# Graph layer kernel on one core: attention's q and k loads regrouped from half blocks to head parities

## The chip, the cores and the metric

The kernel runs on one core of a Trainium2 chip. The metric is the device time of one execution in microseconds (us), lower is better. The kernel before takes 2124.48 us (median of 3 runs, 2124.31 to 2126.77).

## The reference, cut to what matters

There are 6250 nodes with 512 features, 106250 edges sorted by their target, and 64 features per edge. In order:

```python
xn = layernorm(x)
agg = segment_sum(edge_attr, dst) / count            # edges into nodes
gnn = xn + relu(concat(xn, agg) @ W1 + b1) @ W2 + b2
q, k, v = split(xn @ W_qkv.T + b_qkv)                # 8 heads of 64
q, k = sigmoid(q), sigmoid(k)
# i, o, i_hat, o_hat: sums over all nodes of q and k, in two rounds
vw = v * softmax(o_hat, over nodes)
kv = einsum('bshd,bshe->bsde', k, vw)                # per node: heads x heads
r  = einsum('bshd,bsde->bshe', q / i, kv) * sigmoid(i_hat)
x1 = x + gnn + r.reshape(...) @ W_out.T + b_out
out = x1 + gate * expert(layernorm(x1))              # one expert of 16
```

Attention is local to a node: its 8 heads of q meet its own 8 heads of k, an 8x8 matrix per node that is scaled by `mix` (what the softmax, `i` and `i_hat` amount to) and applied to its own v.

## The kernel before, in words

The work goes through six stages one after the other: project (norm, q, k, v and W1's part that needs no edges), norms and scale (the sums over all nodes), attend, gnn, expert. Nodes are handled in 12 full blocks of 512 and a last one of 106 (`TAIL`). Beside the first four stages runs the edge work: SP (SyncE) loads batches of 1024 edges (`Edges.load`, L196, L198, L201: indices, the indices of the whole batch on every partition, attributes), DVE (VectorE) writes selection matrices (L237), PE (TensorE) sums (L249), ACT (ScalarE) copies (L262), and POOL (GpSimd) adds rows into tables in HBM with indirect DMAs of 128 rows (L297), 831 in all. There are 9 buffers (`KEPT`) between ACT and POOL.

Project writes q and k to the HBM tensor `qk_halves`, of shape side (q, k) x 25 half blocks x 128 x 4 chunks x 256 nodes. A feature's chunk is `o`, and the 128 partitions of a chunk are 2 parities `x` of heads times 64 features `d`; one `[o, t]` row of a feature and half block is 4096 contiguous bytes. Norms and scale read it by `load_halves` (L909), one transfer of 1024 KB for each side of a block, with the 128 features outermost on both sides: `rearrange("w p o t -> p w (o t)")`.

Attend (`attend_stage`, L1292) wants another layout. Its tiles `q` and `kk` are `[128, 8, 256]`: partitions 0 to 63 hold feature d of the block's first 256 nodes, partitions 64 to 127 those of the second 256, and the free dimension holds 8 heads (parity x, then chunk o) by 256 nodes. `load_qk` (L1385) fills them with four transfers a block, of 512 KB each: half 0 of q, half 0 of k, half 1 of q, half 1 of k. Each writes 64 partitions, 8192 bytes in each (two rows of 4096, one of either parity). All four count on `qk_in[b % 2]`, and ACT's `by_token` (L1559), which turns k into `kt` with the 8 heads of a node side by side (L1566), waits for the four at once. PE's `scores` (L1485) then multiplies 16 nodes by 16 nodes (128x128) of which DVE's `neighbours` (L1625) keeps the 8x8 blocks on the diagonal, times `mix`; `mixing` (L1509) applies v, and `output` (through `products`, L365) multiplies with W_out in three passes of fp32r. The last block takes TAIL nodes of one half with its own four transfers (L1395), on 64 partitions.

The order of SP's queue in attend is written out by hand (L1445 to L1469). For block b it is: one batch of edges; wait until block b-1 is scored; `load_qk(b + 1)`; wait until block b-1 is mixed; `load_v(b + 1)` (L1401); 16 small transfers for `mix` of block b+1 (L1373), each to 8 partitions, 8 KB in pieces of 32 bytes; the store of block b-1 (L1440); edges; `load_x(b + 1)` (L1411); edges. All of them go through SP's one DMA queue (q1), in order; POOL's indirect DMAs go through q0. Before the loop SP issues `load_qk(0)`, W_out, v of block 0, two biases (L1420, L1421), the stores of `mix` (L1425, L1428) and its first loads, then `load_qk(1)`. The q, k, v, x and mix tiles each have two buffers.

Transfers of the tail block with 106 nodes on the outermost side are L1414 (x), L1443 (store of attend) and L2283 (the last store of the kernel, L2280 for a full block).

Of the kernel before, what the change touches and what calls it, by code (L numbers as in the profile page):

```python
# [17 lines left out]
HDIM = DIM // HEADS  # L18
# [4 lines left out]
CH = DIM // P  # L23
QK = 2 * CH
JH = HID // P
BT = 512
HALF = BT // 2
FULL = TOKENS // BT
TAIL = TOKENS - FULL * BT
# [20 lines left out]
def subtiles(n):  # L50

    return [min(P, n - s) for s in range(0, n, P)]
# [824 lines left out]
def block_at(b):  # L877

    return slice(b * BT, min(TOKENS, (b + 1) * BT))
# [412 lines left out]
def attend_stage(nc, c, edges, before):  # L1292
# [5 lines left out]
    with ExitStack() as ctx:  # L1298
        def sb(what, shape, dt=F32):
            return ctx.enter_context(nc.sbuf_tensor(f"at_{what}", shape, dt))  # L1300
# [4 lines left out]
        def sem(what):  # L1305
            return c.whole.enter_context(nc.semaphore(f"at_{what}"))
# [6 lines left out]
        q, kk, v, x = [[sb(f"{what}0", shape)] for what, shape in  # L1313
                       (("q", [P, HEADS, BT // 2]), ("k", [P, HEADS, BT // 2]), ("v", [P, GROUPS, HDIM]),
                        ("x", [P, CH, DIM]))]
# [23 lines left out]
        mix_in, qk_in, v_in, x_in = [[sem(f"{what}_in{k}") for k in range(2)] for what in ("mix", "qk", "v", "x")]  # L1339
# [27 lines left out]
    def load_mix(b, eng, first, step=2):  # L1367
        part = [i for i, (g0, g1) in enumerate(MIX_PARTS) if g0 <= b * CH < g1][0]
        eng.wait_ge(mix_stored[part], 16)
        rows = c.mix[b * BT:b * BT + sizes[b], :]  # L1370
        for t, g in mix_loads(sizes[b])[first::step]:
            src = rows[t:t + (g - 1) * GT + 1:GT, :].rearrange("g (a h) -> a g h", a=HEADS)
            eng.dma_start(mix[b % 2][t * HEADS:(t + 1) * HEADS, 0:g, t * HEADS:(t + 1) * HEADS], src  # L1373
                          ).then_inc(mix_in[b % 2], 16)
# [8 lines left out]

    def sp_program(sp):
        def load_qk(b):  # L1385
            for half, r in enumerate([BT // 2, BT // 2] if b < FULL else [TAIL]):
                for side, dst in enumerate((q[b % 2], kk[b % 2])):
                    rows = slice(half * HDIM, (half + 1) * HDIM)
                    if r == HALF:
                        sp.dma_start(dst[rows, :, :].rearrange("d (x o) t -> d x (o t)", x=2),  # L1390
                                     c.qk[side, 2 * b + half, :, :, :].rearrange("(x d) o t -> d x (o t)", x=2)
                                     ).then_inc(qk_in[b % 2], 16)
                    else:
                        for x in range(2):
                            sp.dma_start(dst[rows, x * CH:(x + 1) * CH, 0:r],  # L1395
                                         c.qk[side, 2 * b, x * HDIM:(x + 1) * HDIM, :, 0:r]).then_inc(qk_in[b % 2], 16)

        def load_v(b):
            rows = c.v.rearrange("t (h e) -> (t h) e", h=HEADS)
            full = sizes[b] // GT  # L1400
            sp.dma_start(v[b % 2][:, 0:full, :], rows[b * BT * HEADS:b * BT * HEADS + full * P, :]  # L1401
                         .rearrange("(g p) e -> p g e", p=P)).then_inc(v_in[b % 2], 16)
            left = sizes[b] % GT * HEADS
            if left:
                at = b * BT * HEADS + full * P
                sp.dma_start(v[b % 2][0:left, full, :], rows[at:at + left, :]).then_inc(v_in[b % 2], 16)

        def load_x(b):
            n = sizes[b]
            if n == BT:  # L1410
                sp.dma_start(x[b % 2][:, :, :], c.x[block_at(b), :].rearrange("(s p) d -> p s d", p=P)  # L1411
                             ).then_inc(x_in[b % 2], 16)
            else:
                sp.dma_start(x[b % 2][0:n, 0, :], c.x[block_at(b), :]).then_inc(x_in[b % 2], 16)  # L1414

        sp.wait_ge(before.io_mm, EARLY_FREE)
        load_qk(0)
        weights.load(sp)
        load_v(0)
        sp.dma_start(bias[:, :], c.b2.partition_broadcast(P)).then_inc(bias_in, 16)  # L1420
        sp.dma_start(bias_out[:, :], c.b_out.partition_broadcast(P)).then_inc(bias_in, 16)  # L1421
        for i, (g0, g1) in enumerate(MIX_PARTS):
            sp.wait_ge(c.mix_ready, i + 1)
            if (g1 - 1) * P < TOKENS - P:
                sp.dma_start(c.mix[g0 * P:g1 * P, :].rearrange("(s p) f -> p s f", p=P), c.mix_sb[:, g0:g1, :]  # L1425
                             ).then_inc(mix_stored[i], 16)
            else:
                sp.dma_start(c.mix[g0 * P:TOKENS, :], c.mix_sb[0:TOKENS - g0 * P, g0, :]).then_inc(mix_stored[i], 16)  # L1428
            if i == 0:
                load_mix(0, sp, 0)  # L1430
        before.over(sp)
        load_qk(1)
        load_x(0)
        weights.wait(sp)

        def store(b):
            n = sizes[b]
            sp.wait_ge(acc_free, b * CH + len(subtiles(n)))
            if n == BT:
                sp.dma_start(c.base[block_at(b), :].rearrange("(s p) d -> p s d", p=P), done[b % 2][:, :, :]  # L1440
                             ).then_inc(stored[b % 2], 16)
            else:
                sp.dma_start(c.base[block_at(b), :], done[b % 2][0:n, 0, :]).then_inc(stored[b % 2], 16)  # L1443

        for b in range(NB):  # L1445
            batches = share.batches(b)
            for batch in batches[:1]:
                edges.load_ahead(sp, *batch)
            if b + 1 < NB:
                if b:  # L1450
                    sp.wait_ge(scored, b * STEPS)
                    load_qk(b + 1)
                    sp.wait_ge(mixed, b * STEPS)
                else:
                    sp.wait_ge(prepared, 1)
                load_v(b + 1)
                load_mix(b + 1, sp, 0, 1)
            if b:
                store(b - 1)
            for batch in batches[1:2]:  # L1460
                edges.load_ahead(sp, *batch)
            if b + 1 < NB:
                if b:
                    sp.wait_ge(rest_ready, b * CH)
                load_x(b + 1)
            for batch in batches[2:]:
                edges.load_ahead(sp, *batch)
        me.preload(sp)
        store(NB - 1)  # L1469
# [1079 lines left out]
```

## Time and profile before

| | |
|---|---|
| Median of 3 runs | 2124.48 us |
| Profiled execution, its own time | 2126.26 us |
| Its span, first to last instruction | 2124.5 us |
| PE, PEld (weight loads), DVE, POOL, ACT busy | 88%, 71%, 58%, 62%, 26% |
| Mean granted TensorE clock | 0.922 of full speed |
| SP's DMA queue q1, POOL's q0 | 369.74 MB and 28.99 MB |
| q and k loads of attend | 48 transfers of 512 KB |

The profile's page gives busy shares of a whole span; attend is the stretch from about 1094 to 1592 us. "SPq" is time in which SP's queue issues a DMA or is held up in issuing it; a DMA's packets are counted apart, as a share of the time of the core's 16 DMA engines, which can go over 1 where packets of two queues overlap on an engine.

### The profile page before, as it was taken

What the parts mean: (1) busy time and instruction counts of PE and PEld (TensorE: products, weight loads), DVE (VectorE), ACT (ScalarE), POOL (GpSimd) and SP (SyncE); (2) the same over time, 40 slices, a digit from 0 to 9 for tenths busy, and PEclk for the clock granted to TensorE, in tenths of its full rate; (3) what the DMA queues carried; (4) which work ended last, traced back from release to release, by engine and by line L of the source; (5) the groups of instructions that cost most, each with busy time, mean ns of one, the idle gap of its engine ahead of it and who ended that gap; (6) DMA issues with size and microseconds to landing.
All of it is one profiled execution on the core that took longest, in us unless ns stands there. A gap on an engine that the chain in (4) does not pass through costs nothing.

```text
span 2124.5 us, 31099 instructions
## 1 busy us (share of the span) xinstructions
PE 1875.1 (88%) x10776; PEld 1512.1 (71%) x10776; DVE 1222.8 (58%) x3872; ACT 560.4 (26%) x1314; POOL 1325.7 (62%) x850
## 2 busy tenths in 40 slices
PE   2799999999999999788776978888767999998798
PEld 1688888888888888544435767777655888887686
DVE  3643454443443432377855656465648888885575
ACT  1422333223332223111131121212123333333210
POOL 4888888888888888688888787777885000000100
PEclk9999999999999999866586998889887999999899
DMA  9977887777787777799799999999969666653884
GB/s 291 226 158 149 145 157 148 159 148 146 151 158 152 137 133 137 202 233 207 143 307 188 209 195 207 183 210 185 204 133 249 216 212 209 215 180 117 305 292 151
DMA packets 502384, 400.77 MB, mean 189 GB/s; under 512 B 356932, under 2 KB 369476, under 8 KB 502228
## 3 DMA queue, kind: packets, MB, share of 16 engines
q1 hardware_dynamic: 380164, 369.74, 60.5%
q0 software_dynamic: 119952, 28.99, 22.0%
q8 instruction: 86, 1.41, 0.3%
q14 instruction: 70, 0.57, 0.1%
q10 hardware_dynamic: 2112, 0.07, 0.1%
HBM read 244.05 MB, written 154.62 MB: 188 GB/s over the span
## 4 chain that ended last, share of the span: by engine, by line
PE 67%; SPq 17%; DMA 6%; DVE 6%; issue 2%; ACT 1%; POOL 0%; DVEq 0%; POOLq 0%; ACTq 0%
PE pr_out_bank L365 26%; PE gn_acc L365 12%; SPq L1373 9%; PE pr_v_bank L365 7%; PE edge_sum L249 6%; PE ex_y_bank L365 6%; SPq L1390 2%; PE at_acc L365 2%; PE nm_io_bank L872 2%; DMA done<-qk_halves 2%; SPq L196 1%; DVE nm_wide L1093 1%; DMA at_k<-qk_halves 1%; DVE edge_sel L237 1%; PE gn_h L1951 1%
## 5 line engine op out<-in xcount | busy, mean ns | idle before, releaser
L297 POOL DMA_INDIRECT table<-edge_ring,edge_row x831 | 1314.7, 1582 | 309.9 <-issue 226.3
L237 DVE SCALAR_TENSOR_TENSOR edge_sel<-edge_dst_all,edge_dst_f,upper 128x128 f32<-128x128 int16 x831 | 317.3, 438 | 92.3 <-PE edge_sum L249 61.2
L365 PE MATMUL pr_out_bank<-pr_norm_xT_hi,pr_w_hi 128*128 128x512 f32 (+1 forms) x832 | 327.8, 394 | 0.0
L365 PE MATMUL pr_out_bank<-pr_norm_xT_lo,pr_w_hi 128*128 128x512 f32 (+1 forms) x832 | 319.5, 384 | 0.0
L365 PE MATMUL pr_out_bank<-pr_norm_xT_hi,pr_w_lo 128*128 128x512 f32 (+1 forms) x832 | 318.7, 383 | 0.0
L249 PEld LDWEIGHTS edge_sum<-edge_attr,edge_sel 128*128 128x128 f32 x1662 | 236.9, 213 | 110.7 <-DVE edge_sel L237 80.3
L249 PE MATMUL edge_sum<-edge_attr,edge_sel 128*128 128x65 f32 x1662 | 244.3, 297 | 73.4 <-DVE edge_sel L237 71.7
L2292 POOL DMA_INDIRECT ex_w_raw<-in_w_exp,ex_row x4 | 5.2, 1295 | 337.0 <-issue 337.0
L262 ACT ACTIVATE edge_ring<-edge_sum 128x260 f32<-128x260 f32 (+1 forms) x209 | 80.3, 385 | 399.0 <-PE edge_sum L249 311.3
L365 PEld LDWEIGHTS pr_out_bank<-pr_norm_xT_lo,pr_w_hi 128*128 128x128 f32 x832 | 156.7, 188 | 32.1
L365 PEld LDWEIGHTS pr_out_bank<-pr_norm_xT_hi,pr_w_lo 128*128 128x128 f32 x832 | 157.1, 189 | 28.3
L365 PEld LDWEIGHTS pr_out_bank<-pr_norm_xT_hi,pr_w_hi 128*128 128x128 f32 x832 | 157.0, 189 | 27.8
L365 PE MATMUL gn_acc<-gn_w_hi,gn_h_hi 128*128 128x512 f32 (+1 forms) x392 | 155.7, 397 | 0.3 <-DVE gn_h_lo L2096 0.3
L365 PE MATMUL gn_acc<-gn_w_lo,gn_h_hi 128*128 128x512 f32 (+1 forms) x392 | 153.6, 392 | 0.0
L365 PE MATMUL gn_acc<-gn_w_hi,gn_h_lo 128*128 128x512 f32 (+1 forms) x392 | 153.4, 391 | 0.0
L813 DVE TENSOR_TENSOR pr_stage<-pr_v_bank,pr_bias_v 128x512 f32<-128x512 f32 (+1 forms) x49 | 33.9, 692 | 199.4 <-PE pr_v_bank L365 198.6
L1485 PE MATMUL at_s<-at_q,at_kt 64*128 64x128 f32 (+1 forms) x782 | 100.7, 405 | 40.9 <-ACT at_kt L1566 24.5
L764 ACT ACTIVATE pr_stage<-pr_out_bank,bias_qk 128x512 f32<-128x512 f32 (+1 forms) x104 | 68.8, 662 | 211.4 <-PE pr_out_bank L365 189.6
L767 ACT ACTIVATE pr_stage<-pr_out_bank 128x512 f32<-128x512 f32 (+1 forms) x104 | 59.4, 571 | 224.2 <-PE pr_out_bank L365 213.4
L1485 PEld LDWEIGHTS at_s<-at_q,at_kt 64*128 64x128 f32 (+1 forms) x782 | 79.9, 221 | 48.4 <-ACT at_kt L1566 25.9
L485 DVE TENSOR_TENSOR pr_norm_xT_lo<-pr_turn,pr_norm_xT_hi 128x512 fp32r<-128x512 f32 (+1 forms) x49 | 33.8, 689 | 124.4 <-ACT pr_norm_xT_hi L479 112.7
L365 PE MATMUL ex_y_bank<-ex_w_hi,ex_xT_hi 128*128 128x512 f32 (+1 forms) x196 | 77.9, 397 | 14.2 <-DVE ex_w_lo L2388 9.8
(206 smaller groups left out, 3216.2 us busy)
## 6 DMA issues: line engine op xcount, KB each, us to landing
edge_dst_all<-dst SPq DMA_DIRECT2D x103, 256.0 KB
edge_attr<-in_edge_attr SPq DMA_DIRECT2D x103, 256.0 KB
qk_halves<-pr_stage SPq DMA_DIRECT2D x48, 512.0 KB
h_pre_T<-pr_stage SPq DMA_DIRECT2D x48, 512.0 KB
gn_pre<-h_pre_T SPq DMA_DIRECT2D x48, 512.0 KB, 6.7
done<-qk_halves SPq DMA_DIRECT2D x16, 1024.0 KB
table<-edge_ring,edge_row POOLq DMA_INDIRECT x831
pr_norm_x<-in_x SPq DMA_DIRECT2D x12, 1024.0 KB
```

Of the source, the lines that this page charges most:

```text
L237: op = dve.scalar_tensor_tensor(out=self.sel[q][0:rows, j, 0:rows], in0=self.dst_all[k][0:rows, t:t + m * (rows - 1) + 1:m], scalar=self.d ...
L249: mm = pe.matmul(self.p_sum[q][0:rows, j * ECOLS:(j + 1) * ECOLS], self.sel[q][0:rows, j, 0:rows], self.attr[k][0:rows, j0 + j, :], start= ...
L262: act.activation(self.sums[g % KEPT][0:rows, j0:j0 + w, :], self.p_sum[q][0:rows, 0:w * ECOLS] .rearrange("p (w c) -> p w c", w=w), ACT.Co ...
L297: pool.indirect_dma_start(self.c.table[t], bass.IndirectOffsetOnAxis(ap=self.row[k][0:rows, j:j + 1], axis=0), self.sums[k][0:rows, j, :], ...
L365: mm = pe.matmul(out, a, c, start=first and i == 0, stop=last and i == n - 1)
L764: act.activation(kept, by_half(out_bank[e % 2][:, 0:n]), ACT.Sigmoid, bias=c.bias_qk[:, i:i + 1], accum_out=part[k][:, i:i + 1]).then_inc( ...
L767: act.activation(pair[p % RING][:, e % 2, 0:n], out_bank[e % 2][:, 0:n], ACT.Copy).then_inc(out_free, 1)
L813: dve.tensor_tensor(v[0:r, i, :], v_bank[i % 2][0:r, :], bias_v[0:r, :], ALU.add).then_inc(v_bank_free, 1)
L872: mm = pe.matmul(out[j * ROWS:(j + 1) * ROWS, 0:n], c.heads[:, side * CH + j, :], x[j], start=side == 0, stop=side == 1)
L1373: eng.dma_start(mix[b % 2][t * HEADS:(t + 1) * HEADS, 0:g, t * HEADS:(t + 1) * HEADS], src).then_inc(mix_in[b % 2], 16)
L1390: sp.dma_start(dst[rows, :, :].rearrange("d (x o) t -> d x (o t)", x=2), c.qk[side, 2 * b + half, :, :, :].rearrange("(x d) o t -> d x (o ...
L1485: mm = pe.matmul(s_bank[half][0:w * HEADS, j * P:j * P + w * HEADS], kt[u][rows, t:t + w, :].rearrange("d t h -> d (t h)"), q[b % 2][rows, ...
```

## The change

The four transfers of a full block are cut differently. Before, a transfer took one half block and both parities of heads and wrote 64 partitions; after, it takes one parity and both half blocks and writes 128 partitions, 4096 bytes in each. There are still four transfers of 512 KB, 512 rows of 4096 bytes in all, the same bytes at the same places, the same semaphore and counts. They are issued in the order q parity 0, q parity 1, k parity 0, k parity 1. The source pattern's outermost dimension is now the half block `w`, of size 2, then 64 features, then 4096 contiguous bytes; on the destination's side the outermost is the 128 partitions. The tail's transfers move the same pieces as before, in the new order.

```diff
     def sp_program(sp):
         def load_qk(b):
-            for half, r in enumerate([BT // 2, BT // 2] if b < FULL else [TAIL]):
-                for side, dst in enumerate((q[b % 2], kk[b % 2])):
-                    rows = slice(half * HDIM, (half + 1) * HDIM)
-                    if r == HALF:
-                        sp.dma_start(dst[rows, :, :].rearrange("d (x o) t -> d x (o t)", x=2),
-                                     c.qk[side, 2 * b + half, :, :, :].rearrange("(x d) o t -> d x (o t)", x=2)
+            for side, dst in enumerate((q[b % 2], kk[b % 2])):
+                for x in range(2):
+                    rows, chunks = slice(x * HDIM, (x + 1) * HDIM), slice(x * CH, (x + 1) * CH)
+                    if b < FULL:
+                        sp.dma_start(dst[:, chunks, :].rearrange("p o t -> p (o t)"),
+                                     c.qk[side, 2 * b:2 * b + 2, rows, :, :].rearrange("w d o t -> w d (o t)")
                                      ).then_inc(qk_in[b % 2], 16)
                     else:
-                        for x in range(2):
-                            sp.dma_start(dst[rows, x * CH:(x + 1) * CH, 0:r],
-                                         c.qk[side, 2 * b, x * HDIM:(x + 1) * HDIM, :, 0:r]).then_inc(qk_in[b % 2], 16)
+                        sp.dma_start(dst[0:HDIM, chunks, 0:TAIL],
+                                     c.qk[side, 2 * b, rows, :, 0:TAIL]).then_inc(qk_in[b % 2], 16)
```

## Rows read from the trace of the kernel before

**Rows 1.** Busy time by windows, all of attend (us; then engines, clock, DMA share, GB/s).

```profile
core 0: us, PE busy (x) PEld busy (x) DVE busy (x) ACT busy (x) POOL busy (x), PEclk, DMA share, GB/s
1130.00:1533.00 403.00, 335.09 (x3032) 283.50 (x3032) 242.45 (x788) 86.03 (x118) 323.19 (x204) 0.87 1.04 198
```

**Rows 2.** The chain that ended last, one block of attend (start us, us, what).

```profile
1281.50 12.75 DMA at_k<-qk_halves
1294.27 1.93 ACT at_kt L1566
1296.25 2.11 PE at_s L1485 x16
1298.36 7.24 PE at_acc L365 x24
...
1315.52 15.22 SPq L1373
```

**Rows 3.** SP's queue in order of time, one block (start us, us).

```profile
1277.02 3.14 SPq L1390 DMA_DIRECT2D at_q<-qk_halves  x1
1280.20 0.61 SPq L1390 DMA_DIRECT2D at_k<-qk_halves  x1
1280.85 0.61 SPq L1390 DMA_DIRECT2D at_q<-qk_halves  x1
1281.50 0.61 SPq L1390 DMA_DIRECT2D at_k<-qk_halves  x1
1282.56 0.70 SPq L1401 DMA_DIRECT2D at_v<-v_rows  x1
1283.31 19.02 SPq L1373 DMA_DIRECT2D at_mix<-mix_rows  x16
...
1308.48 0.75 SPq L201 DMA_DIRECT2D edge_attr<-in_edge_attr  x1
```

**Rows 4.** One tile's instructions, q loads: issue ns, first and last start.

```profile
L1390 SPq DMA_DIRECT2D at_q<-qk_halves x24: 607/626/3613, 1093.7 to 1504.9; - x24
```

**Rows 5.** Busy time by windows, that block's q and k transfer (columns as rows 1).

```profile
1283.00:1295.00 12.00, 9.55 (x156) 8.23 (x152) 8.87 (x31) 2.20 (x4) 9.18 (x7) 0.99 1.10 216
```

**Rows 6.** DMA view of 1277 to 1300 us: POOL's queue, packets, MB, share of 16 engines.

```profile
q0 software_dynamic: 1825, 0.42, 23.9%
```

**Rows 7.** Busy time by windows, 106-row store alone at the kernel's end (columns as rows 1).

```profile
2119.00:2123.50 4.50, 0.00 (x0) 0.00 (x0) 0.00 (x0) 0.00 (x0) 0.00 (x0) 0.71 0.13 41
2120.00:2121.00 1.00, 0.00 (x0) 0.00 (x0) 0.00 (x0) 0.00 (x0) 0.00 (x0) 0.94 0.13 39
2121.00:2122.00 1.00, 0.00 (x0) 0.00 (x0) 0.00 (x0) 0.00 (x0) 0.00 (x0) 0.50 0.13 45
2122.00:2123.00 1.00, 0.00 (x0) 0.00 (x0) 0.00 (x0) 0.00 (x0) 0.00 (x0) 0.50 0.13 51
```

**Rows 8.** DMA view of 2005 to 2030 us, GB/s in 40 slices of expert's 128-partition transfers.

```profile
GB/s 262 370 387 396 403 413 410 403 328 374 410 410 397 397 396 396 406 167 52 23 279 360 380 239 216 206 311 410 403 410 302 315 413 403 347 39 0 121 380 360
```

**Rows 9.** One tile's instructions, the last store: issue ns min/median/max of 128 and 106 rows.

```profile
L2280 SPq DMA_DIRECT2D out<-ex_done x12: 372/377/378, 1997.8 to 2114.7; - x12
L2283 SPq DMA_DIRECT2D out<-ex_done x1: 259/259/259, 2117.5 to 2117.5; - x1
```

**Rows 10.** SP's queue in order of time, attend's beginning (start us, us).

```profile
1093.67 0.62 SPq L1390 DMA_DIRECT2D at_q<-qk_halves  x1
...
1097.87 15.71 SPq L1420 DMA_DIRECT2D at_bias<-in_b  x1
1113.63 0.43 SPq L1421 DMA_DIRECT2D at_rest<-in_b_out  x1
1114.11 0.43 SPq L1425 DMA_DIRECT2D mix_rows<-done  x1
1118.91 3.58 SPq L1373 DMA_DIRECT2D mix<-mix_rows  x8
```

**Rows 11.** Busy time by windows, gnn's first blocks (columns as rows 1).

```profile
1600.00:1640.00 40.00, 31.91 (x119) 24.05 (x120) 33.34 (x52) 13.44 (x28) 25.62 (x17) 0.80 0.96 228
```

**Rows 12.** Busy time by windows, loads of qk_halves by 128 partitions in norms (columns as rows 1).

```profile
880.00:895.00 15.00, 8.19 (x47) 2.79 (x47) 3.10 (x14) 1.71 (x3) 4.21 (x3) 0.71 1.08 384
```

## The prediction

> **What bounds the kernel now.** I read the page first: PE is busy 88% of the span, but the change touches attend alone, so I went to that stage. There (by windows) PE is busy 335 of 403 us, and the DMA engines' share is 1.04 [rows 1]: PE has slack and the DMA engines have none. Next the chain that ended last: through a block of attend it goes over the wait for q and k to land (12.75 us) to `kt`, the scores and the output, and back into SP's queue, held up 15.2 us at the first of the small `mix` loads [rows 2]. Then SP's own queue in order of time: from 1277.02 to 1309.23 us it is issuing or held up nearly without a gap, and the longest piece is the `mix` loads, 19.0 us for 16 of them, the first of which alone holds the queue 11.8 us (19.0 less 15 issues of 0.4 to 0.6 us, 7.2 in all) [rows 3]. It comes free at 1295, within a us of the time at which q and k have landed, 1281.50 + 12.75 = 1294.25 [rows 2, 3]. So the reader is to see a stage that goes at the pace of SP's queue, and that queue stands still once a block while q and k move. The second q issue of block 5 is at 1280.85 us [rows 3], that of block 11, the last of the 24, at 1504.9 [rows 4]: (1504.9 - 1280.85)/6 = 37.3 us a block.
>
> What q and k cost today: 4 x 512 KB are 2.10 MB a block. While they move, the core moves 216 GB/s [rows 5], so they take at least 2.10 MB / 216 GB/s = 9.7 us; from the first issue's end to landing it is 1294.25 - 1280.16 = 14.1 us [rows 2, 3]. I take 10: POOL's packets, in between (23.9% of the engines' time [rows 6]), have to be moved before and after as well.
>
> **What the change does, part by part.**
>
> Instructions: four issues before, four after; the order q, q, k, k in place of q, k, q, k changes nothing, as ACT waits for all four, and PE reads q after `kt`. The tail block moves the same pieces. These are zero, with no cover needed.
>
> The shape. A transfer now has 128 partitions on the SBUF side, but its source begins with a dimension of size 2 (the half blocks), where every large transfer of the kernel before has 64 rows or more there. What a small or awkward outer size does is to be seen in the tail's transfers of 106 rows. The last store of the kernel, 212 KB from 106 partitions, runs with nothing beside it, and in each window the DMA share is 0.13, which is 2 of 16 engines; the rate ends at 51 GB/s [rows 7]. Full transfers of 128 rows reach 413 GB/s [rows 8], that is 25.8 on each of 16, and 51 is twice that. Its issue is shorter too, 259 against 377 ns [rows 9]. So a transfer is dealt out over as many engines as divide its outer dimension: 106 = 2 x 53 gives 2. The trace has no large transfer whose two sides disagree. I take it that the smaller side decides, because equal shares must be cut on both sides at once and the source, 2 x 64 rows with a jump between, has only two outer pieces. Then all four transfers go over the same two engines. The Trainium skill says so outright (DMA: Bandwidth & Descriptors, "Why a DMA increments its semaphore by 16 and not by 1"): the engines used are the largest number up to 16 that divides the slowest dimension of both sides. The trace agrees for 106 rows (share 0.13); no run here shows it yet for sides that differ.
>
> The price: 2.10 MB at 51 GB/s are 41.1 us a block. The bounds: at the best slice's rate that any 16 engines reach, 413, two engines give 52 and 40.6 us; at the whole lone store's mean, 41 GB/s [rows 7], it is 51.1 us. I take 41.1: the mean of 41 holds the slow beginning (39), and q and k, ten times as long, have nearly all their time behind it. What is added to a block lies between 40.6 - 14.1 = 26.5 and 51.1 - 9.7 = 41.4; I take 41.1 - 10 = 31.
>
> What covers it: nothing that I can find. Behind the four stand v, 16 `mix` loads, the store, edges and x in the same queue, and SP is held up until the q and k transfers have drained. The other 14 engines would have time, but the queue is in order. The two engines also carry their sixteenths of all else (v, x, store, edges, POOL's rows) and the `mix` loads. That work is in the 37.3 us of today's period, and I leave it where it is: 37.3 - 10 + 41.1 = 68.4 us a block. The double buffers don't help: they hide latency, and here a resource is full. PE, with 30.9 us a block (335 over 10.8 blocks), DVE and POOL have room in 68 us, so no engine becomes the bound.
>
> Whether all 12 loads count: block 0's are issued at 1093.67, and behind them the bias load is held up 15.7 us, so that the first `mix` store goes out at 1114.1 and the first `mix` load at 1118.9 [rows 10]. That hold grows by 31 as well, and the stage's start is behind it. Blocks 1 to 11 pay in the loop. 12 x 31 = 372 us.
>
> What comes back: in gnn's first 40 us PE is busy 31.9, and POOL still works off its rows (25.6 of 40) [rows 11]. With a longer attend POOL has no backlog left, and up to 8 us return. I take 5.
>
> The sum: the profiled execution's own 2126.3 + 372 - 5 = 2493 us (its span is 2124.5; it is 1.8 us above the median of the three runs, within their spread). Every block's cost can be at a bound: 12 x 26.5 gives 2439, 12 x 41.4 gives 2618.
>
> **The rivals.**
>
> *All 16 engines and twice the rate (faster).* If the outer 2 does not restrict it, the change does what its words say. The same tensor, loaded by 128 partitions, moves at 384 GB/s [rows 12], against 216 by 64 partitions [rows 5]: q and k would take 5.5 us in place of 9.7, and the hold at the first `mix` load would be 4.2 us shorter. SP's queue is the pace, so it is a gain for each block, 12 x 4.2 = 50 us: 2076 us. For it: the two rates differ by nearly two, with the same bytes in the same 4096-byte rows. Against it: the 2. It decides wherever the engines in use are more than about 8 (at 25.8 GB/s each, 8 would equal today's 216). The skill has this rule too (SBUF — State Buffer, "Door 1: The DMA port swizzle"): partitions 0 to 63 reach 8 of 16 ports, and the two rates agree with it [rows 5, 12]. Chance 0.08.
>
> *Two engines, but other work slips past (slower by less).* If SP is not held up by the drain, v, x and stores move on 14 engines meanwhile, and POOL's rows overlap with q and k on the two. Then the period tends to the two engines' own load: 41 us plus what of their other work cannot overlap. Today all work fills 1.04 of the period, 38.7 us, 10 of it q and k; if a third of the other 28.7 overlaps, it is 41 + 19 = 60, which adds 23 a block: 2126 + 276 - 5 = 2397. For it: the share above 1 shows overlap exists. Against it: the hold that ends with the landing [rows 2, 3]. Chance 0.15.
>
> *Two engines, and nothing overlaps (slower by more).* The same hold, with POOL's rows and the rest of an engine's queue taking turns with q and k packet by packet, so that the rate of the two is the 41 GB/s of the store's mean or less: 2618 us. For it: POOL takes 23.9% today. Against it: POOL's rows per block stay the same, and are in the 37.3 already. Chance 0.10.
>
> *No difference.* It needs a number of engines near 8, or a hidden load; the chain speaks against hidden [rows 2]. Chance 0.01.
>
> **How the numbers follow.** The forecast has what is left, 0.66, and gives 2493 us. What a measurement of this kernel can tell from no change is about 0.2%, 4 us. The range runs from the lower two-engine case to nearly the upper, 2390 to 2600: it leaves out the gain (0.08), the even case (0.01), about 0.05 below the lower case and 0.06 at the top. Slower 0.91, faster 0.08, same 0.01.
>
> **What would show it.** In the profile after: the q load's issues 68 us apart in place of 37; in attend 2 MB drained at some 50 GB/s with a DMA share well below 1 while they do (near 0.13 plus POOL's); the first issue behind v held up some 43 us; the issues of the q and k loads shorter than their 607 ns of before [rows 4], as 259 is to 377; the wait for q and k the longest of ACT's and, through ACT, of PE's; stages before 1090 us unchanged. It is wrong if the transfers of q and k run at over 200 GB/s, or if the q loads' spacing is far from 68: below 60 other work has slipped past, above 75 the drain takes turns.

## The result, and the profile after

The changed kernel takes 2523.8 us (median of 4 runs, 2520.23 to 2527.05) against 2125.62 us: a ratio of 1.186 (95% interval 1.182 to 1.190). The forecast was 2493, range 2390 to 2600. The profiled execution took 2526.46 us for a span of 2524.7, which is 400 us more than before.

The first thing to find is where the 400 us are. The instructions of one tile, the q tile of attend, in the changed kernel (issue ns min/median/max, first and last start in us):

```profile
L1390 SPq DMA_DIRECT2D at_q<-qk_halves x24: 538/1730/3864, 1098.6 to 1868.7; - x24
```

From the first to the last of the 24 it is 770.1 us, against 411.2 [rows 4]: 359 us more over 11 blocks, 32.6 a block. Ahead of the first it is 4.9 us more; behind the last one, 656.0 against 619.6, 36 more, nearly all of it the last full block's own load. The 4.9 need no part of the change: in the other runs, whose code ahead of attend is the same, attend's first q load is issued between 1093.9 and 1101.4 us. So attend has the rest, 395 us. Busy time by windows, attend after (us, engines, clock, DMA share, GB/s), to be held against [rows 1]:

```profile
1170.00:1933.00 763.00, 345.60 (x3038) 292.25 (x3036) 242.78 (x792) 85.48 (x118) 340.12 (x214) 0.68 0.53 106
```

PE has about the same work (346 us against 335) in 763 us in place of 403, and the DMA share has fallen from 1.04 to 0.53: everything waits and nothing is full on average. What is full shows in the DMA view of 1325 to 1360 us, in which q and k move (GB/s in 40 slices):

```profile
GB/s 46 77 45 77 49 78 44 75 51 67 60 57 65 50 72 51 75 45 49 40 49 52 51 56 47 64 225 224 181 186 233 185 83 52 51 51 51 51 51 51
```

51 GB/s is the very rate of the last store on its two engines [rows 7]. In a stretch with nothing beside them the DMA share is also that of two engines of 16, 0.13 (busy time by windows, columns as rows 1):

```profile
1355.00:1360.00 5.00, 0.00 (x0) 0.00 (x0) 0.00 (x0) 0.00 (x0) 0.00 (x0) 0.50 0.13 52
```

What stands above 51 is POOL's rows and, for 6 us, v. By the packet records, 896 of v's 1024 packets start between 1347.7 and 1354 us, and the last 128 between 1360 and 1366.1: 14 engines do their part at once, and the two that hold q and k do theirs behind them. SP's queue in order of time in that block, the counterpart of [rows 3]:

```profile
1311.40 3.37 SPq L1390 DMA_DIRECT2D at_q<-qk_halves  x2
1314.81 21.20 SPq L1390 DMA_DIRECT2D at_k<-qk_halves  x2
1336.58 10.29 SPq L1400 DMA_DIRECT2D at_v<-v_rows  x1
1346.92 25.34 SPq L1373 DMA_DIRECT2D at_mix<-mix_rows  x16
...
1378.84 5.78 SPq L1390 DMA_DIRECT2D at_q<-qk_halves  x2
```

The one hold of 11.8 us has become four: the queue takes the two q transfers and is then held in the first transfer of k (9.3 us), the second (11.9), v (10.3) and the first `mix` load (17.4). Who waits (us in total, times, longest), 1170 to 1933 us:

```profile
ACT at_kt L1565 <- DMA at_k<-qk_halves: 401.5, 11, 39.6
PE at_s L1484 <- ACT at_kt L1565: 335.6, 10, 36.3
...
DVE at_near L1624 <- DMA at_mix<-mix_rows: 217.4, 6, 43.9
DVE at_near L1624 <- DMA mix<-mix_rows: 203.1, 5, 41.9
```

The last two are one wait in two buffers, 420 us together, longer than the wait for q and k. In this block `kt` starts when k has landed, but `near` only 12 us later, when `mix` has (ACT's and DVE's instructions in order of time; in brackets the idle time before and what ended it):

```profile
1362.56 1.92 ACT L1565 ACTIVATE at_kt<-at_k 128x1024 f32<-128x1024 f32 x1 [37.29 <-DMA at_k<-qk_halves]
1374.50 1.29 DVE L1624 TENSOR_TENSOR at_near<-at_s,at_mix 128x512 f32<-128x512 f32 x2 [43.02 <-DMA at_mix<-mix_rows]
```

So what arrives last in a block is not q and k but what stands behind them in SP's queue.

### The profile page after: what moved, and what is told of

The parts are those of the page before. It is cut to its first block and busy times, and to the rows that moved or that the text cites. A ratio compares the mean times of both kernels' runs of the same rounds, so it can differ in the third digit from the quotient of the medians.

```text
span 2524.7 us, 31099 instructions
## 1 busy us (share of the span) xinstructions
PE 1889.8 (75%) x10776; PEld 1521.4 (60%) x10776; DVE 1222.2 (48%) x3872; ACT 559.8 (22%) x1314; POOL 1326.5 (53%) x850
## 3 DMA queue, kind: packets, MB, share of 16 engines
q1 hardware_dynamic: 379492, 369.73, 48.9%
## 5 line engine op out<-in xcount | busy, mean ns | idle before, releaser
L249 PE MATMUL edge_sum<-edge_attr,edge_sel 128*128 128x65 f32 x1662 | 244.4, 297 | 69.6 <-DVE edge_sel L237 69.6
L1565 ACT ACTIVATE at_kt<-at_k 128x1024 f32<-128x1024 f32 (+1 forms) x25 | 48.0, 1920 | 442.5 <-DMA at_k<-qk_halves 442.5
L1624 DVE TENSOR_TENSOR at_near<-at_s,at_mix 128x512 f32<-128x512 f32 x48 | 30.9, 685 | 228.8 <-DMA at_mix<-mix_rows 217.4
L1624 DVE TENSOR_TENSOR at_near<-at_s,mix 128x512 f32<-128x512 f32 (+1 forms) x50 | 32.0, 681 | 220.7 <-DMA mix<-mix_rows 209.8
```

The lines of the kernel that those rows point to most:

```text
L249: mm = pe.matmul(self.p_sum[q][0:rows, j * ECOLS:(j + 1) * ECOLS], self.sel[q][0:rows, j, 0:rows], self.attr[k][0:rows, j0 + j, :], start= ...
L1565: act.activation(kt[u][0:rows, 0:r, :].rearrange("d t (o x) -> d t o x", x=2), kk[b % 2][0:rows, :, u * P:u * P + r].rearrange("d (x o) t ...
L1624: op = dve.tensor_tensor(near[step % 2][half][:, 0:whole, :], s_bank[half][:, 0:whole * P].rearrange("p (j f) -> p j f", f=P), mix[b % 2][ ...
```

## The experiments

A packet length below is the mean duration of the 512 packets of 4096 bytes that a block's q and k make, from the trace's packet records over six blocks (3 to 8, counted from 0); a spacing is the mean distance of a block's first q issue from the next block's over the same six. Before they are 0.308 us and 37.0 us; after, 0.172 and 69.6. Where a run changes the number of transfers in a block, the count that ACT waits for is changed with it; the diffs here leave such lines out.

**One transfer for each half block.** The change's cut stays, without the dimension of 2:

```diff
-                        sp.dma_start(dst[:, chunks, :].rearrange("p o t -> p (o t)"),
-                                     c.qk[side, 2 * b:2 * b + 2, rows, :, :].rearrange("w d o t -> w d (o t)")
-                                     ).then_inc(qk_in[b % 2], 16)
+                        for w in range(2):
+                            sp.dma_start(dst[w * HDIM:(w + 1) * HDIM, chunks, :].rearrange("p o t -> p (o t)"),
+                                         c.qk[side, 2 * b + w, rows, :, :].rearrange("d o t -> d (o t)")
+                                         ).then_inc(qk_in[b % 2], 16)
```

> The change's cut by parity stays, but each transfer is made in two, one for each half block: 8 transfers a block, 64 partitions and 64 source rows outermost, 4096 bytes in each. Theory (a source with an outermost dimension of 2 goes over two engines, and nothing else of the change costs): all 16 engines again, so near the kernel before, 2126 to 2150 us (four more issues of 0.6 us a block), q and k packets near 0.3 us each, block spacing 37 to 39 us. Rival (the cut itself costs: one row of 4096 bytes a partition, parities apart, the order q, q, k, k): near the changed kernel, 2480 us or more.

Measured: 2104.64 us (5 runs), ratio 0.991 (0.988 to 0.994). The rival is out: the cut costs nothing. But it is also faster than the kernel before, which I had not expected, with packets of 0.255 us and a spacing of 35.3.

**62 and 2 partitions.** The kernel before, whose transfers have no jump between half blocks, with each cut at an awkward row:

```diff
-                        sp.dma_start(dst[rows, :, :].rearrange("d (x o) t -> d x (o t)", x=2),
-                                     c.qk[side, 2 * b + half, :, :, :].rearrange("(x d) o t -> d x (o t)", x=2)
-                                     ).then_inc(qk_in[b % 2], 16)
+                        for d0, d1 in ((0, 62), (62, HDIM)):
+                            sp.dma_start(dst[half * HDIM + d0:half * HDIM + d1, :, :].rearrange("d (x o) t -> d x (o t)", x=2),
+                                         c.qk[side, 2 * b + half, :, :, :].rearrange("(x d) o t -> d x (o t)", x=2)[d0:d1]
+                                         ).then_inc(qk_in[b % 2], 16)
```

> The kernel before with its own cut, but each transfer of 64 partitions is made in two, of 62 and of 2 partitions: no outermost dimension of 2 with a jump behind it, but counts that 16 does not share a factor above 2 with. Theory (the number of engines is the largest up to 16 that divides the outermost count): two engines for all of q and k, so near the changed kernel, 2500 to 2570 us, spacing near 70 us. Rival (it was the jump between the two half blocks, or the 128 partitions, that made the transfers slow): near the kernel before, 2126 to 2160 us.

Measured: 2561.59 us (one run), spacing 72.3. A slowdown of about the change's size (437 us against 398), without the change. Its DMA view, 1330 to 1365 us (GB/s in 40 slices), shows the same floor, 40 to 51:

```profile
GB/s 75 45 83 40 101 45 77 50 71 51 67 55 64 63 53 70 49 78 41 82 45 78 45 78 49 45 44 49 47 51 51 51 56 47 143 233 197 170 135 145
```

**61 and 3 partitions.** The same, cut elsewhere:

```diff
-                        for d0, d1 in ((0, 62), (62, HDIM)):
+                        for d0, d1 in ((0, 61), (61, HDIM)):
```

> As the run with 62 rows, but cut in 61 and 3 partitions: 61 is prime. Theory (largest divisor up to 16): 95% of the bytes go over one engine, 2.0 MB at 24 to 25.5 GB/s are 78 to 83 us, so the spacing is 37.3 - 10 + 80 = 107 and more, about 2126 + 12 x 72 = 2990, between 2920 and 3080 us. Rival (a slow kind of transfer, whatever its count): as with 62 rows.

Measured: 2984.65 us (one run), spacing 107.9. The DMA view, 1450 to 1500 us (GB/s in 40 slices), and busy time in a window of it:

```profile
GB/s 23 62 46 24 24 21 26 26 26 26 26 26 26 26 26 26 23 26 26 26 26 26 39 26 23 26 26 26 26 26 26 26 23 26 26 26 26 26 39 161
...
1460.00:1495.00 35.00, 0.00 (x0) 0.00 (x0) 0.00 (x0) 0.00 (x0) 0.00 (x0) 0.50 0.07 26
```

26 GB/s is half of 51, and a share of 0.07 is one engine of 16. With 16, 2 and 1 engines for nearly all of the same bytes the spacing is 37.0, 72.3 and 107.9 us. The number of engines comes from the outer count: 64 gives 16, 62 gives two and 61 one. For the changed kernel it comes from the side with the 2, although the other has 128, as the run without the 2 shows. Whether that is because 2 is the smaller of the two or the largest divisor that both share, no run here can tell, as 2 divides 128.

**q by the change's cut, k by the old one.**

```diff
-                    if b < FULL:
+                    if b < FULL and side == 1:
+                        sp.dma_start(dst[rows, :, :].rearrange("d (x o) t -> d x (o t)", x=2),
+                                     c.qk[side, 2 * b + x, :, :, :].rearrange("(x d) o t -> d x (o t)", x=2)
+                                     ).then_inc(qk_in[b % 2], 16)
+                    elif b < FULL:
```

> q by the change's cut, k by the cut of before: half of the bytes over two engines. Theory (SP's in-order queue pays for the drain of the two engines): the drain is 22 us for q and 5 for k on those two, in place of 10, so about 16.5 us a block: 2126 + 12 x 16.5 = 2324, between 2290 and 2360 us. Rival (it is the wait of kt for k that costs, not the queue; q is needed later): 2126 to 2200 us.

Measured: 2335.5 us (one run), spacing 54.0, half of what the change adds (211 of 398 us). k's issues are held for it (min/median/max ns):

```profile
L1390 SPq DMA_DIRECT2D at_k<-qk_halves x24: 608/5150/9996, 1096.7 to 1705.9; - x24
```

The cost goes by the bytes on the two engines, and it is there with q alone on them, so that it isn't k's wait as such.

**v from ACT's queue.** The changed kernel, with v of blocks 2 and later moved, to see whether the order of SP's queue or the two engines are what is short:

```diff
-                load_v(b + 1)
+                if not b:
+                    load_v(sp, b + 1)
...
+            if 0 < b < FULL:
+                act.wait_ge(mixed, b * STEPS)
+                load_v(act, b + 1)
```

> The changed kernel, with v of blocks 2 and later loaded from ACT's queue in place of SP's. Theory (the two engines are full: of 69.5 us a block they spend 44 on q and k and some 22 on the rest of SP's transfers): v stays on the same engines, and what it gains is at most its overlap, 0 to 5 us a block: 2465 to 2525 us. Rival (the cost is SP's order alone, 14 engines would take v meanwhile and the period would fall by v's whole hold of 6 to 11 us): 2400 to 2450 us.

Measured: 2512.76 us, ratio to before 1.182 (1.177 to 1.186), spacing 68.4 against 69.6. It gives back 11 us of 398, about 1 us a block. But v doesn't go beside q and k here: ACT issues it 3 us ahead of them. ACT's queue and SP's, in order of time (start us, us):

```profile
1308.64 0.69 ACTq L1387 DMA_DIRECT2D at_v<-v_rows  x1
...
1311.85 6.59 SPq L1400 DMA_DIRECT2D at_q<-qk_halves  x2
1318.49 22.29 SPq L1400 DMA_DIRECT2D at_k<-qk_halves  x2
1340.89 28.18 SPq L1373 DMA_DIRECT2D at_mix<-mix_rows  x16
```

So the run shows that v's place in SP's queue is worth about 1 us a block: with v gone from it, the `mix` loads are held longer (28.2 us in place of 25.3), and the queue is held until q and k have drained all the same. What v would gain beside the drain it doesn't show.

**Half 1 from ACT's queue.** This and the next five runs look into the gain of the first one. The kernel before, with its own cut; in blocks 2 to 11 half 1 goes from ACT:

```diff
+                    load_qk(sp, b + 1, (0,))
...
+            if 0 < b < FULL - 1:
+                act.wait_ge(scored, b * STEPS)
+                load_qk(act, b + 1, (1,))
```

> The kernel before with its own cut; for blocks 2 to 11 the transfers of half 1 (partitions 64 to 127) are issued from ACT's queue at the start of its part of the block, those of half 0 from SP's, so that both halves of the partitions are written at the same time by all 16 engines. Theory (64 partitions are slow because all engines write to one half of the memory at a time; 0.31 us a packet against 0.17 by 128): packets fall from 0.31 toward 0.2 us, SP's hold is 3 to 5 us shorter in 10 blocks: 2075 to 2100 us. Rival (no gain by the mix of partitions, or ACT's queue is held up in issuing and delays the copies behind it): 2120 to 2160 us.

Measured: 2132.1 us (12 runs), ratio 1.004 (1.002 to 1.006), packets 0.297 us. The rival's number, but the trace shows that the case was not made: the two halves were not in flight side by side. ACT's queue in order of time, in one block (start us, us):

```profile
1277.98 0.59 ACTq L1389 DMA_DIRECT2D at_q<-qk_halves  x1
1278.60 0.97 ACTq L1389 DMA_DIRECT2D at_k<-qk_halves  x1
```

SP's queue in the same block:

```profile
1285.97 4.88 SPq L1389 DMA_DIRECT2D at_q<-qk_halves  x1
1290.89 0.61 SPq L1389 DMA_DIRECT2D at_k<-qk_halves  x1
```

ACT issues some 8 us earlier; SP is still at its edge loads, one of which holds it 5.4 us. By the packet records half 1's packets run from 1282.3 to 1289.4 us and half 0's from 1292.6 to 1299.5: half 0 begins when half 1 is done. So this run says nothing for or against the theory; the order of transfers in one queue is what the next runs change.

**The eight transfers, halves grouped.** Only the order differs from the first run: w outermost.

```diff
-            for side, dst in enumerate((q[b % 2], kk[b % 2])):
-                for x in range(2):
...
-                        for w in range(2):
+            for w, side, x in [(w, s, x) for w in range(2 if b < FULL else 1) for s in range(2) for x in range(2)]:
```

> The same 8 transfers of 64 partitions as in the run with one half each (2104.6 us, packets 0.255 us), in another order: the four of half 0 first, then the four of half 1. Theory (a run of transfers to the same 64 partitions is slow, and alternation lets an engine's next packet go to the other half): packets back to 0.29 to 0.31 us, 2118 to 2135 us. Rival (smaller transfers or single rows of 4096 bytes are what helped): 2100 to 2110 us.

Measured: 2131.02 us for the profiled execution, packets 0.306 us; two of the four times were far off (2434 and 6167 us, for which no cause was found), so the same kernel was run again.

> The kernel of the grouped run again, 8 transfers with half 0's four first, as two of its four times were far off (2434 and 6167 us beside 2123 and 2131). Theory (alternation is what helps): 2118 to 2135 us, packets 0.30 us. Rival (smaller transfers help): 2100 to 2110 us.

Measured: 2127.26 us (10 runs), ratio 1.0025 (1.000 to 1.005), packets 0.303 us. The same eight transfers take 2105 us when the halves alternate and 2127 when they don't. So the gain of the first run comes from the order, and not from the size of the transfers. ACT's idle time before `kt`, from the view of the k tile's instructions (us, times), is in the first run:

```profile
  DMA at_k<-qk_halves: 31.3, 10
```

and in the grouped one, run again:

```profile
  DMA at_k<-qk_halves: 46.8, 12
```

**Four transfers, halves alternating.** The kernel before with its two loops swapped:

```diff
-            for half, r in enumerate([BT // 2, BT // 2] if b < FULL else [TAIL]):
-                for side, dst in enumerate((q[b % 2], kk[b % 2])):
+            for side, dst in enumerate((q[b % 2], kk[b % 2])):
+                for half, r in enumerate([BT // 2, BT // 2] if b < FULL else [TAIL]):
```

> The kernel before with its own four transfers, in the order q half 0, q half 1, k half 0, k half 1 in place of q, k, q, k of half 0 and then of half 1. Theory (alternation of the partition halves): part of the gain, as a transfer is 32 packets an engine and the halves meet only at its ends: packets 0.27 to 0.30 us, 2108 to 2122 us. Rival (only size matters): 2120 to 2130 us, as before.

Measured: 2117.86 us (10 runs), ratio 0.995 (0.993 to 0.998), packets 0.296 us: a small gain, from order alone. (The expectation's 32 packets an engine is that of all four transfers; a transfer has 128 rows, 8 for an engine.)

**Sixteen transfers, halves alternating.**

```diff
-                        for w in range(2):
-                            sp.dma_start(dst[w * HDIM:(w + 1) * HDIM, chunks, :].rearrange("p o t -> p (o t)"),
+                        for d, w in ((0, 0), (0, 1), (32, 0), (32, 1)):
+                            sp.dma_start(dst[w * HDIM + d:w * HDIM + d + 32, chunks, :].rearrange("p o t -> p (o t)"),
```

> As the run with one half each, but every transfer is cut again at feature 32: 16 transfers of 128 KB and 32 partitions, the halves alternating. Theory (alternation, finer: 2 packets an engine in a row in place of 4): packets 0.19 to 0.24 us and 2 to 4 us a block less for them, but SP has 8 more issues of 0.6 us, 4.9 us a block, which its hold covers only as long as there is one (10 us a block in that run): 2085 to 2110 us. Rival (issue time decides): 2115 to 2160 us.

Measured: 2095.01 us (4 runs), ratio 0.9865 (0.982 to 0.991), packets 0.205 us, spacing 34.4. This beats both kernels. These transfers alternate more finely and are also smaller; sixteen with the halves grouped was not tried, so the step from eight to sixteen isn't shown to be order alone. Its SP queue in one block (start us, us):

```profile
1298.41 6.33 SPq L1391 DMA_DIRECT2D at_q<-qk_halves  x8
1304.78 3.69 SPq L1391 DMA_DIRECT2D at_k<-qk_halves  x8
...
1309.80 14.61 SPq L1373 DMA_DIRECT2D mix<-mix_rows  x16
```

Busy time by windows while q and k move (us, engines, clock, DMA share, GB/s), 291 GB/s where it was 216 [rows 5]:

```profile
1304.00:1312.00 8.00, 8.00 (x93) 6.72 (x93) 4.58 (x14) 0.96 (x2) 6.78 (x4) 0.90 1.16 291
```

**Thirty-two transfers.** The same with 16 partitions each:

```diff
-                        for d, w in ((0, 0), (0, 1), (32, 0), (32, 1)):
+                        for d, w in [(d, w) for d in range(0, HDIM, 16) for w in range(2)]:
```

> 32 transfers of 64 KB and 16 partitions, halves alternating: one packet an engine in a row. Theory: packets 0.17 to 0.20 us, little below the 0.205 of 16 transfers, while SP has 16 more issues of about 0.5 us, 8 us a block, and its holds were only some 7 us a block there: the queue's issue time becomes the bound, 2100 to 2150 us. Rival (finer is always better): 2080 to 2092 us.

Measured: 2170.79 us (4 runs), ratio 1.0215 (1.018 to 1.025), spacing 40.5. The direction is the theory's, but the time is 21 us above its range of 2100 to 2150, and one reason in it failed: packets are 0.239 us, longer than with 16, not 0.17 to 0.20. The queue:

```profile
1301.98 10.56 SPq L1391 DMA_DIRECT2D at_q<-qk_halves  x16
1312.59 8.80 SPq L1391 DMA_DIRECT2D at_k<-qk_halves  x16
...
1322.35 12.66 SPq L1373 DMA_DIRECT2D at_mix<-mix_rows  x16
```

SP now spends 19.4 us on q and k where 16 transfers need 10.0, and of that the `mix` loads give back 2. That is 7 us a block; the spacing grew by 6.1, and 12 blocks of that are 73 of the 76 us between the two runs. Why the packets got longer again stays open; each transfer also writes to 16 partitions only, and that wasn't tried apart.

## Why the prediction was right, point by point

- **The bound.** That the stage goes at the pace of SP's queue is borne out from both sides: a longer drain comes out in the block's spacing nearly in full (half the bytes, half the cost), and so does a longer issue time with 32 transfers. What lands last in a block is `mix`, which stands behind q and k in that queue, and not k.
- **Two engines.** Right. The step that the trace of before could not show, that the side with the 2 decides where the other has 128, is shown by the changed kernel's 51 GB/s and share of 0.13, and by its cost going away when the 2 does; 62 and 61 rows, which give two engines and one with the old cut, show that it is the count. The prediction's own words for it, the smaller side, fit these runs, but so does a divisor that both share. The rule of the Trainium skill (DMA: Bandwidth & Descriptors, "Why a DMA increments its semaphore by 16 and not by 1") is the second of these, the largest number up to 16 that divides the outermost count of both sides, and it held in each of these runs.
- **The price a block.** Forecast 31 us, measured 32.6 (q issues of 12 blocks). Both of its terms were too small. The first of the 4096-byte packets starts 3.5 to 5.8 us behind the first issue, and the last ends 50.4 to 53.1 behind it, so that the drain is about 47 us and not 41.1: POOL's rows take 13.4% of the engines' time in the view of 1325 to 1360 us, and the packets are 0.172 us long where 51 GB/s would give 0.161. By the same measure it was 12.8 us before, not 10. The difference of the two is 34, of which 32.6 came out; where the rest went was not tried apart. That 31 came so near is in part luck: the two terms were short by 5.9 and 2.8 us, and as one is taken from the other, half of the larger error went out again.
- **The cover.** Forecast as none. Nearly right: v's other 14 shares do slip past, visible as the hump of 181 to 233 GB/s, but v is not complete before the two engines have done theirs, 12 us later. Taking v out of SP's queue brought 1 us a block. The rival with 23 us a block falls with the measured 32.6 and with SP's holds, which were there as forecast.
- **The number of blocks.** 12 was right. Block 0's counts as well: the changed kernel issues the first `mix` store at 1155.47 us, against 1114.1 [rows 10], and 4.9 of the 41 us between them were there before attend began. Block 0 so paid 36.
- **What comes back.** The 5 us were not seen: from the tail block's first q load to the end it is 591.9 us, against 591.1 before. In gnn's first 40 us PE is busy 33.1 against 31.9 [rows 11], with POOL idle, so that POOL's backlog was not what held those blocks:

```profile
2000.00:2040.00 40.00, 33.14 (x125) 24.39 (x126) 33.57 (x53) 13.42 (x28) 0.00 (x0) 0.83 0.76 210
```

- **The sum.** 372 - 5 forecast, 400 in the profiled execution: 12 blocks at 1.6 more are 19, the 5 that did not come back, 5 ahead of attend, where runs of the same code differ by more, and the last block's 4 above the others' 32.6.
- **The signs named beforehand.** Spacing 68, measured 69.6; the rate is as forecast. Two signs were wrong in form. The issues of q and k did not become shorter than 607 ns: of q only the shortest is (538; the median is 1730), and those of k take 8302 ns and more, since the queue's hold moved into them. And the hold of 43 us, forecast for the first issue behind v, is 17.4 there: it begins three transfers earlier and comes to 48.9 us over the four.
- **The rival on the other side** was wrong for the change, and what it says of 64 partitions is borne out. They are slow to write to when all engines do it at once: alternating the halves brings the packets from 0.306 to 0.255 us with nothing else changed, and sixteen transfers gain some 30 us of the 50 that it offered. With 62 rows, where two engines do nearly all of the work, the packets to one half take 0.183 us, against 0.308 with 16. The Trainium skill's rule (SBUF — State Buffer, "Door 1: The DMA port swizzle"), that partitions 0 to 63 reach 8 of the 16 ports, agrees with these times; ports themselves are in no trace.

## What to carry to other kernels

Look at the outermost dimension of both sides of a transfer, not only at the partitions: one small or awkward count (here a 2 on the source's side, 62 or 61 on both) takes it from 16 engines to two or one, and in an in-order queue everything behind it waits. Where tiles fill the partitions by halves, let the transfers alternate between the halves, and try how fine they can get before the queue's issue time costs more: here 8 gave 0.9% and 16 gave 1.4% (ratio 0.9865), and 32 lost 2%. A DMA share of 0.5 can hide two engines that are full.

## What the runs showed of the hardware that was not expected

- The order of transfers in one queue changes the length of single packets. By how many packets an engine gets in a row for the same half, if a transfer's packets are shared equally by 16 engines: 16 (four or eight transfers, grouped) 0.308 and 0.306 us (0.303 when run again), 8 (four alternating) 0.296, 4 (eight) 0.255, 2 (sixteen) 0.205, 1 (thirty-two) 0.239. At equal size, order alone was varied for 16 against 4 (eight transfers) and for 16 against 8 (four).
- How far SP runs ahead depends on what is queued. Of transfers with 64 rows for an engine (128 rows on two) two were accepted and the next held the queue about 10 us each; of those with 8 (128 rows on sixteen) it took all four, three of them in 0.6 us each [rows 3].
- One engine reaches 26 GB/s and two reach 51, with packets of 0.170 and 0.172 us: neither gets faster for being nearly alone. The 4096-byte packets of norms' loads to 128 partitions [rows 12], on a core that moves 384 GB/s, have a mean of 0.166.
- A transfer that goes over all 16 engines, queued behind one that holds two of them, is done by the other 14 at once and by the two 12 us later (v's 896 and 128 packets).
